# Layer 2 of a graph network: gathered rows added by VectorE into PSUM instead of by TensorE

## The chip, the cores and the metric

One NeuronCore of a Trainium2 chip runs the whole program. The metric is the time of one execution on the device in microseconds (us). All tensors are float32 unless said otherwise.

## The reference, cut to what matters

Four graph layers run one after the other on 3125 nodes of width 64, with 100000 edges that are sorted by destination. The change is inside layer 2:

```
xs = x[start]                                   # source row of each edge
h  = relu(concat(xs, x[end]) @ We1 + be1)       # 100000 x 128
e  = sigmoid(h @ We2 + be2)                     # one gate per edge
m  = e * xs                                     # message, width 64
m_sum = segment_sum(m, end);  m_max = segment_max(m, end)
... a small network on the nodes: (m_max, m_sum, x) -> x_out
```

## The kernel before, in words

**Layout.** The padded edges lie as 128 partitions x T = 784 columns, and a partition's edges are consecutive. A group is K = 8 columns, so there are NG = 98 groups. Loops over groups are written by `quads` (L127): six groups in line, then a loop whose body holds four groups, so that buffer numbers are constants.

**What layer 2 needs per edge.** The product with We1 is taken per node beforehand: the table `tab2` has, for each node, its source half of the product (128 wide) and the row itself (64 wide), and `put2` has the destination half, non-zero only at the first edge of each destination. Four groups of buffers rotate: `g2` for gathered rows (8 x 192), `z2` for destination rows (8 x 128).

**The engines in layer 2, for group g with slot s = g % 4:**

- SyncE (SP queue): `load_group` (L624) loads the ring of indices, waits until group g-4's destination rows are filled and added (`filled2`, `summed2`), and loads `z2` (L633, 512 KB); then `load2` (L634) clears part of layer 3's table (L491, 1040 KB).
- GpSimd: `gather2` (L802) waits for the ring, `summed2` and `made2` of group g-4, and issues eight indirect DMAs (L718), one column of 128 rows each.
- VectorE: `edges2` (L2260) is one stretch per group. For each of the eight columns k it runs `fill` (L1790), which spreads the destination's row to all its edges: z[k] = z[k-1] * ns + z[k], 128 wide, in SBUF; then one piece of older work: `relu2` of group g-2 after column 1 (L2231), `reduce2` of group g-2 after column 3 (L2238), and for each column the two instructions of `sum2` of group g-3 (L2252 and L2256, the running sum and maximum of the messages, 64 wide).
- TensorE: `add_up` (L1357) adds the gathered and the filled rows into two banks of PSUM by two products with the identity each (L1366, L1367), after `got` (gather landed), `filled2` and `work2`.
- `relu2` reads that sum from PSUM, applies relu, multiplies by we2 and writes `pr2` in SBUF; `reduce2` sums it to one score per edge.
- ScalarE: `gate` (L1039) applies the sigmoid (L1045), then writes the eight messages `m2` to SBUF (L1048), 64 wide each, and raises `made2`. It also stores the running sums (`keep2`, L1037).

Each instruction of VectorE is preceded by register and wait instructions on its own sequencer: `Beats` (L93) computes the value waited for, and `mark` computes the address of the column's marker. These show in the trace as DVEq.

**The order around the change.** VectorE's program is one fixed order per group, as listed. A slot comes free for GpSimd when ScalarE's messages of group g-4 are out. Softmax semaphores of layer 3 (`total_in`, `logged`, `inverse`) exist only there.

Of the kernel before, what the change touches and what calls it, by code (L numbers as in the profile page):

```python
# [21 lines left out]
ALU = mybir.AluOpType  # L22
# [6 lines left out]
P = 128  # L29
# [125 lines left out]
def gnn_program(nc, x, src, dst, etype, adj_v, deg_v, w0, b0, deg_coeff, coeff_param, scale_param,  # L155
# [3 lines left out]
    with ExitStack() as ctx:  # L159
# [176 lines left out]
        g2, z2, hold2 = quad(0, W2), quad(6200, HID), area(10300, HID)  # L336
        pr2, e2, m2, st2 = area(10500, K, HID), area(11600, 4, K), pair(11700, D), pair(12800, 2 * D)
        agg2 = area(17100, NT, 2 * D)
# [58 lines left out]
        apart1 = sem("apart1")  # L397
        filled2, summed2, work2, gate2, made2, scan2 = (sem(n) for n in ("filled2", "summed2", "work2", "gate2", "made2", "scan2"))
        filled3, summed3, work3, scored = (sem(n) for n in ("filled3", "summed3", "work3", "scored"))
# [3 lines left out]
        soft_in, soft_exp = sem("soft_in"), sem("soft_exp")  # L403
        total_in, logged, inverse = sem("total_in"), sem("logged"), sem("inverse")
        c_tail, c_turn, c_scan, c_back, c_in = (sem(n) for n in ("c_tail", "c_turn", "c_scan", "c_back", "c_in"))
# [105 lines left out]
        def _(sp):  # L511
# [111 lines left out]

            def load_group(n, put_rows, rows, filled_to, summed, g, s, uses):  # L624

                again = not isinstance(g, int) or g >= 4
                ring_load(n, g, s, *(((got[s], (uses[0] + past(n, s)) * 16 * K),) if again else ()))
                if again:
                    sp.wait_ge(filled_to, (g - 3) * K + 1)
                    sp.wait_ge(summed, g - 3)  # L630
                    if n == "3a":
                        sp.wait_ge(work3, (g - 4) * STEPS3 + READS3)
# [19 lines left out]

            quads(sp, lambda g, s, uses: load_group("3a", put3, z3, filled3, summed3, g, s, uses))

# [15 lines left out]
        def _(pool):  # L670
# [170 lines left out]
        def _(act):  # L841
# [259 lines left out]
            for r in range(H):  # L1101
                act.wait_ge(total_in, r + 1)
                act.activation(inv3[:, r, :], f3[:, r, :], ACT.Ln).then_inc(logged, 1)
            for r in range(H):
                act.wait_ge(logged, r + 1)
                act.activation(inv3[:, r, :], inv3[:, r, :], ACT.Exp, scale=-1.0).then_inc(inverse, 1)

# [15 lines left out]
        def _(pe):  # L1123
# [233 lines left out]
            def add_up(n, rows_of, banks, per_bank, width, g, s, uses, filled, steps, used, each, reads, summed):  # L1357
# [127 lines left out]
        def _(dve):  # L1485
# [737 lines left out]
            dve.wait_ge(hold_in, 16 * (PIECES + 2))  # L2223
            fills2, beats2, scans2 = Beats(dve, filled2, K), Beats(dve, work2, 2), Beats(dve, scan2, 2 * K)
# [15 lines left out]
            def sum2(g, s, uses, k):  # L2240

                h = s % 2
                if k == 0:
                    scans2.group(g)
                    dve.wait_ge(made2, g + 1)
                    if late(g, 2):
                        before = (s - 2) % 4
                        dve.wait_ge(states_out[before], (before_of(g, s, uses, 2)[0] + (1 + states_before(1, before))) * 16)
                start = isinstance(g, int) and g == 0 and k == 0
                prior = st2[:, h, k - 1, :] if k else st2[:, 1 - h, K - 1, :]  # L2250
                scans2.wait(1 if k else 0)
                scans2.add(dve.scalar_tensor_tensor(out=st2[:, h, k, 0:D], in0=zero[:, 0:D] if start else prior[:, 0:D],  # L2252
                                                    scalar=mark(ns, g, k), in1=m2[:, h, k, :],
                                                    op0=ALU.mult, op1=ALU.add))
                scans2.wait(1)
                scans2.add(dve.scalar_tensor_tensor(out=st2[:, h, k, D:2 * D], in0=lowest[:, :] if start else prior[:, D:2 * D],  # L2256
                                                    scalar=mark(neg, g, k), in1=m2[:, h, k, :],
                                                    op0=ALU.add, op1=ALU.max))
# [13 lines left out]
            for g in range(NG - 3, NG):  # L2272
                if g > NG - 3:
                    relu2(g, g % 2)
                    reduce2(g, g % 2)
# [142 lines left out]
            def total_done(r):  # L2418
                step(dve.tensor_scalar(f3[:, r, :], f3[:, r, :], 1e-16, None, ALU.max))
                dve.sem_inc(total_in, 1)  # L2420

            head_totals(6, "max", rest_of_maximum, neg, neg_last, late3, from_maximum)
            head_totals(10, "sum", sum_forward, ns, nl, first_last[:, :], total_done)
            for r in range(H):
                dve.wait_ge(inverse, r + 1)
                step(dve.tensor_tensor(f3[:, r, :], f3[:, r, :], inv3[:, r, :], ALU.mult))
# [103 lines left out]
```

## Time and profile before

| | us |
|---|---|
| median of 3 runs | 7645.4 |
| range of the runs | 7613.19 to 7655.54 |
| the profiled execution's own time | 7577.06 |
| its span | 7575.3 |
| layer 2's edge loop, from the first gather to the last message sum | 4207.6 to 5583.1 |

Over the span VectorE is busy for 3908.5 us (52%), GpSimd 3549.2 (47%), TensorE 2801.8 (37%) and ScalarE 1046.5 (14%). The numbers are of one execution of the program, recorded by the profiler. Times inside are counted from the start of the span. The loop over layer 2's edges takes about 18% of the span.

### The profile page before, as it was taken

The page shows a single profiled execution, that of the slowest core. Times are in us where ns is not written, and L with a number is a line of the kernel's source. Part 1 is how long each engine was busy: PE and PEld are TensorE (multiplying, and loading weights), DVE is VectorE, ACT ScalarE, POOL GpSimd, SP SyncE. Part 2 cuts the span into 40 slices and gives each one's busy share as a digit, 9 for nine tenths or more (in the row PEclk, how much of TensorE's full clock was granted, in tenths as well). Part 3 has the DMA queues.
Part 4 walks back from the last instruction along what each step waited for, and adds up shares of the span by engine and source line. Part 5 has one row for each costly group of instructions (what it writes and reads, how often), then busy time and mean ns, then how long its engine had stood idle before and what let it go on. Part 6 is the DMA issues. An engine that isn't in the chain of part 4 may idle for free. (4 is left out here: it accounts for less than half of the span.)

```text
span 7575.3 us, 62622 instructions
## 1 busy us (share of the span) xinstructions
PE 2801.8 (37%) x10703; PEld 1391.0 (18%) x10703; DVE 3908.5 (52%) x10542; ACT 1046.5 (14%) x2423; POOL 3549.2 (47%) x3645
## 2 busy tenths in 40 slices
PE   2116200057710000192002344333445655665694
PEld 1114100012300000181001111111122222222232
DVE  4218200399700000199865465555545666667995
ACT  0000000012200000181253111111110000000332
POOL 5650577400177777500002655555536666665463
PEclk9999999987755555596555677667677788787897
DMA  8100000045331111100242666666637777776693
GB/s 314 44 22 9 14 1 0 0 174 218 133 92 48 48 47 48 31 0 0 82 149 76 209 215 214 202 200 211 216 108 239 245 247 249 249 247 224 221 333 111
DMA packets 458410, 1039.70 MB, mean 137 GB/s; under 512 B 129581, under 2 KB 247829, under 8 KB 428140
## 3 DMA queue, kind: packets, MB, share of 16 engines
q1 hardware_dynamic: 167594, 579.38, 21.6%
q0 software_dynamic: 131968, 217.09, 10.5%
q10 hardware_dynamic: 158658, 241.42, 9.1%
q14 instruction: 159, 1.30, 0.1%
q8 instruction: 31, 0.51, 0.0%
HBM read 559.03 MB, written 476.15 MB: 137 GB/s over the span
## 5 line engine op out<-in xcount | busy, mean ns | idle before, releaser
L718 POOL DMA_INDIRECT arena<-tab,ring x2352 | 2334.7, 993 | 1345.8 <-issue 1104.9
L1366 PE MATMUL psum<-arena,ident 128*128 128x512 f32 x1176 | 760.1, 734 | 1369.5 <-DVE arena L1796 1198.0
L1796 DVE SCALAR_TENSOR_TENSOR arena<-arena,ns 128x64 f32<-128x64 f32 (+2 forms) x2351 | 874.6, 372 | 451.3 <-issue 304.2
L760 POOL DMA_INDIRECT weights<-arena x784 | 788.9, 1006 | 365.7 <-issue 312.7
L1941 DVE SCALAR_TENSOR_TENSOR arena<-iota_row,base,psum 128x200 f32<-128x200 f32 x784 | 278.4, 419 | 1082.1 <-remote 566.3
L1367 PE MATMUL psum<-arena,ident 128*128 128x512 f32 x1176 | 695.3, 677 | 0.0
L1330 PE MATMUL psum<-agg,arena 128*128 128x200 bf16 x2352 | 261.8, 267 | 1048.5 <-issue 623.0
L1366 PEld LDWEIGHTS psum<-arena,ident 128*128 128x128 f32 x1176 | 257.5, 234 | 1763.8 <-issue 1264.1
L2355 DVE SCALAR_TENSOR_TENSOR arena<-psum,rowb 128x1024 f32<-128x1024 f32 x196 | 239.0, 1219 | 375.7 <-remote 363.0
L707 POOL DMA_INDIRECT put<-arena,zidx x75 | 73.5, 979 | 739.2 <-DVE arena L1909 630.5
L1330 PEld LDWEIGHTS psum<-agg,arena 128*128 128x128 bf16 x2352 | 210.0, 104 | 1086.7 <-issue 627.4
L1448 PE MATMUL psum<-arena,ident 128*128 128x512 f32 x784 | 362.1, 608 | 54.0 <-DVE arena L2447 53.7
L830 POOL TENSOR_TENSOR arena<-arena,score 128x256 f32<-128x256 f32 x294 | 232.4, 815 | 249.3 <-issue 124.1
L1585 DVE SCALAR_TENSOR_TENSOR arena<-psum,arena,upper 128x128 bf16<-128x128 f32 x784 | 227.2, 348 | 224.6 <-remote 183.9
L1367 PEld LDWEIGHTS psum<-arena,ident 128*128 128x128 f32 x1176 | 264.0, 225 | 364.5 <-issue 364.5
L1748 DVE TENSOR_TENSOR nodev<-psum,nodev 128x25 f32<-128x25 f32 x98 | 17.4, 177 | 549.9 <-remote 445.0
L1240 PE MATMUL psum<-arena 128*128 128x25 bf16 x784 | 38.4, 185 | 683.3 <-DVE arena L1758 540.6
L735 POOL DMA_INDIRECT arena<-betas,eidx x25 | 24.9, 998 | 567.7 <-DVE score L2128 557.4
L2256 DVE SCALAR_TENSOR_TENSOR arena<-arena,neg 128x64 f32<-128x64 f32 x783 | 219.3, 280 | 130.2 <-issue 122.4
L937 ACT ACTIVATE psum<-psum,own_row 128x512 f32<-128x512 f32 x196 | 129.8, 662 | 1116.1 <-remote 716.9
L2252 DVE SCALAR_TENSOR_TENSOR arena<-arena,ns 128x64 f32<-128x64 f32 x783 | 221.1, 282 | 120.1 <-issue 92.9
L2362 DVE TENSOR_REDUCE arena<-arena 128x8 f32<-128x512 f32 x392 | 265.8, 679 | 0.1
(431 smaller groups left out, 4685.8 us busy)
## 6 DMA issues: line engine op xcount, KB each, us to landing
put<-zero SPq DMA_DIRECT2D x98, 1040.0 KB
arena<-put SPq DMA_DIRECT2D x98, 1040.0 KB
spill<-arena ACTq DMA_DIRECT2D x98, 1024.0 KB
arena<-spill SPq DMA_DIRECT2D x98, 1024.0 KB
state<-arena ACTq DMA_DIRECT2D x147, 512.0 KB
weights<-zero SPq DMA_DIRECT2D x32, 1600.0 KB
arena<-weights SPq DMA_DIRECT2D x32, 1600.0 KB, 7.3
put<-zero SPq DMA_DIRECT2D x14, 3584.0 KB
```

The lines of the kernel that those rows point to most:

```text
L718: pool.indirect_dma_start(out=rows[:, h, k, :], out_offset=None, in_=table[:, :], in_offset=bass.IndirectOffsetOnAxis(ap=ring[:, h, word + ...
L760: pool.indirect_dma_start(out=weights0[:, :], out_offset=bass.IndirectOffsetOnAxis(ap=words0[:, g, k:k + 1], axis=0), in_=words0f[:, g, K ...
L830: message = pool.tensor_tensor(y3[:, s % 2, k, :].rearrange("p (h c) -> p h c", c=D), gc3[:, s, k, 0:HD].rearrange("p (h c) -> p h c", c=D ...
L1330: mm = pe.matmul(bank(2 + 2 * h + k // 2)[:, k % 2 * NT * R:(k % 2 + 1) * NT * R], lhsT=picks[:, h, k, :], rhs=s_parts[:, a, :], start=(a ...
L1366: pe.matmul(place, lhsT=ident[:, :], rhs=rows_of[0][:, s, columns, 0:width], start=True, stop=False)
L1367: mm = pe.matmul(place, lhsT=ident[:, :], rhs=rows_of[1][:, s, columns, 0:width], start=False, stop=True)
L1448: mm = pe.matmul(bank(h).rearrange("p (c k) -> p k c", k=K), lhsT=ident[:, :], rhs=y3[:, h, :, head * D:(head + 1) * D], start=(head == 0) ...
L1585: marked = dve.scalar_tensor_tensor(out=alike[:, h * 4 + k, :], in0=bank(h)[:, k * P:(k + 1) * P], scalar=key[:, column], in1=upper[:, :], ...
L1796: beats.add(dve.scalar_tensor_tensor(out=rows[:, s, k, :], in0=before, scalar=mark(ns, g, k), in1=rows[:, s, k, :], op0=ALU.mult, op1=ALU. ...
L1941: pick = dve.scalar_tensor_tensor(out=sifted[:, h * 4 + k, :], in0=iota_row[:, :], scalar=src_column[:, column], in1=bank(2 + 2 * h + k // ...
L2355: beats3.add(dve.scalar_tensor_tensor(out=pr3[:, columns, :], in0=bank(4 * h + 2 * part, 2).rearrange("p (k c) -> p k c", c=HD), scalar=0. ...
L2362: beats3.add(dve.tensor_reduce(rs3[:, columns, :], pr3[:, columns, :].rearrange("p k (h c) -> p k h c", c=D), AX.X, ALU.add))
```

## The change

TensorE takes no part in layer 2's loop any more. `fill2` writes the filled destination rows to PSUM (`ends2_up`, two banks for even and two for odd groups), taking the previous row from there too. `add2`, at the head of `edges2`, waits for the gather (`got`) and writes gathered + filled rows of group g-2 to `pr2`, which is now in PSUM (two banks). `relu2` works on `pr2` in place, `reduce2` reads it there. The messages `m2` are in PSUM as well, one bank for each parity. `summed2` is gone, SyncE waits for `filled2` of group g-4 alone, ScalarE waits for `scan2` before it writes messages. Three semaphores of layer 3's softmax are folded into two others with other counts.

```diff
+        ends2_up = [bank(2 * h, 2).rearrange("p (k c) -> p k c", c=HID) for h in range(2)]
+        m2 = [bank(4 + h).rearrange("p (k c) -> p k c", c=D) for h in range(2)]
+        pr2 = bank(6, 2).rearrange("p (k c) -> p k c", c=HID)
...
             def load2(g, s, uses):
-                load_group("2", put2, z2, filled2, summed2, g, s, uses)
+                load_group("2", put2, z2, g, s, uses, (filled2, (g - 3) * K))
...
             def gather2(g, s, uses):
                 ready((ring_in[s], (uses[0] + past("2", s)) * 16 + 16),
-                      *(((summed2, g - 3), (made2, g - 3)) if not isinstance(g, int) or g >= 4 else ()))
+                      *(((made2, g - 3),) if not isinstance(g, int) or g >= 4 else ()))
...
-                act.wait_ge(work2, g * 2 + 2)
+                act.wait_ge(work2, g * 3 + 3)
                 act.activation(e2[:, 2 + h, :], e2[:, h, :], ACT.Sigmoid, bias=par[:, 6:7]).then_inc(gate2, 1)
                 act.wait_ge(gate2, g + 1)
+                if not isinstance(g, int) or g >= 2:
+                    act.wait_ge(scan2, (g - 1) * 2 * K)
                 for k in range(K):
-                    message = act.activation(m2[:, h, k, :], g2[:, s, k, HID:W2], ACT.Copy, scale=e2[:, 2 + h, k:k + 1])
+                    message = act.activation(m2[h][:, k, :], g2[:, s, k, HID:W2], ACT.Copy, scale=e2[:, 2 + h, k:k + 1])
...
-            quads(pe, lambda g, s, uses: add_up("2", (g2, z2), 2, 4, HID, g, s, uses, filled2, K, work2, 2, 1, summed2))
...
-            def relu2(g, h):
+            def add2(g, s, use):
                 beats2.group(g)
                 beats2.wait()
-                dve.wait_ge(summed2, g + 1)
-                beats2.add(dve.scalar_tensor_tensor(out=pr2, in0=bank(2 * h, 2).rearrange("p (k c) -> p k c", c=HID), scalar=0.0,
-                                                    in1=spread(row["we2"].unsqueeze(1), P, K, HID), op0=ALU.max, op1=ALU.mult))
+                dve.wait_ge(got[s], (use + past("2", s)) * 16 * K + 16 * K)
+                beats2.add(dve.tensor_tensor(pr2, g2[:, s, :, 0:HID], ends2_up[s % 2], ALU.add))
+            def relu2():
+                beats2.wait()
+                beats2.add(dve.scalar_tensor_tensor(out=pr2, in0=pr2, scalar=0.0, in1=spread(row["we2"].unsqueeze(1), P, K, HID),
+                                                    op0=ALU.max, op1=ALU.mult))
...
+            def fill2(g, s, k):
+                h = s % 2
+                if k == 0:
+                    fills2.group(g)
+                fills2.wait()
+                before = ends2_up[h][:, k - 1, :] if k else hold2 if isinstance(g, int) and g == 0 else ends2_up[1 - h][:, K - 1, :]
+                fills2.add(dve.scalar_tensor_tensor(out=ends2_up[h][:, k, :], in0=before, scalar=mark(ns, g, k), in1=z2[:, s, k, :],
+                                                    op0=ALU.mult, op1=ALU.add))
             def edges2(g, s, uses):
+                if late(g, 2):
+                    add2(g - 2, (s - 2) % 4, before_of(g, s, uses, 2)[0])
+                    beats2.wait()
                 dve.wait_ge(loaded[s], uses[0] * 16 + 16 * (1 + after("2", s)))
                 for k in range(K):
-                    fill(fills2, z2, hold2, g, s, k)
+                    fill2(g, s, k)
                     if late(g, 2) and k == 1:
-                        relu2(g - 2, s % 2)
+                        relu2()
```

In `sum2`, `in1` becomes `m2[h][:, k, :]` in both instructions; the three groups after the loop call `add2` and `relu2` for g > NG - 3.

## Rows read from the trace of the kernel before

**Rows 1.** Windows: us, busy (instructions) of PE, PEld, DVE, ACT, POOL; PEclk, DMA, GB/s.

```profile
4224.00:5584.00 1360.00, 519.21 (x785) 200.71 (x783) 779.82 (x2533) 227.25 (x882) 739.72 (x771) 0.69 0.61 205
4862.40:4869.00 6.60, 6.00 (x8) 2.07 (x7) 6.60 (x23) 2.17 (x9) 5.05 (x6) 0.62 0.41 139
4869.00:4885.00 16.00, 3.69 (x8) 1.44 (x8) 2.29 (x8) 0.15 (x1) 10.14 (x11) 0.77 0.88 294
4885.00:4891.80 6.80, 0.37 (x1) 0.38 (x2) 6.78 (x23) 2.32 (x9) 0.00 (x0) 0.50 0.09 30
4458.20:4461.00 2.80, 2.80 (x4) 1.21 (x4) 0.00 (x0) 0.00 (x0) 2.19 (x3) 0.50 0.57 203
4461.00:4469.20 8.20, 2.77 (x6) 1.07 (x5) 7.73 (x26) 2.32 (x9) 5.77 (x7) 0.92 0.73 227
```

**Rows 2.** Lines by form, 4300 to 5500: xcount, busy, mean ns, idle before, releasers.

```profile
L718 POOL DMA_INDIRECT arena<-tab,ring x684 | 656.5, 960 | 544.2 <-issue 542.4 <-PE psum L1367 1.8
L1796 DVE SCALAR_TENSOR_TENSOR arena<-arena,ns 128x128 f32<-128x128 f32 x691 | 239.8, 347 | 239.7 <-issue 236.9 <-DVE arena L2256 1.8
L2252 DVE SCALAR_TENSOR_TENSOR arena<-arena,ns 128x64 f32<-128x64 f32 x691 | 195.1, 282 | 98.9 <-issue 82.3 <-DVE arena L1796 10.3 <-DVE arena L2231 2.7
L1048 ACT ACTIVATE arena<-arena 128x64 f32<-128x64 f32 x688 | 173.5, 334 | 2.8
L2231 DVE SCALAR_TENSOR_TENSOR arena<-psum,rowb 128x1024 f32<-128x1024 f32 x86 | 105.1, 1222 | 44.8 <-issue 42.5
L2238 DVE TENSOR_REDUCE arena<-arena 128x8 f32<-128x1024 f32 x86 | 104.4, 1213 | 14.5 <-issue 12.4 <-DVE arena L1796 2.1
```

**Rows 3.** Waits, 4300 to 5500: waiter, releaser, total us, times, longest.

```profile
ACT arena L1045 <- DVE arena L2238: 860.2, 72, 19.7
POOL arena L718 <- issue: 542.4, 678, 12.3
POOL arena L718 <- PE psum L1367: 1.8, 6, 0.3
```

**Rows 4.** Timeline, 4881 to 4892: start, us, instruction, idle before.

```profile
4881.24 0.95 POOL L718 DMA_INDIRECT arena<-tab,ring  x1 [0.30 <-issue]
4885.02 1.23 DVE L2231 SCALAR_TENSOR_TENSOR arena<-psum,rowb 128x1024 f32<-128x1024 f32 x1 [1.75 <-issue]
4887.47 1.21 DVE L2238 TENSOR_REDUCE arena<-arena 128x8 f32<-128x1024 f32 x1
4888.72 0.30 ACT L1045 ACTIVATE arena<-arena,par 128x8 f32<-128x8 f32 x1 [19.57 <-DVE arena L2238]
4889.05 2.02 ACT L1048 ACTIVATE arena<-arena 128x64 f32<-128x64 f32 x8
4891.84 1.00 POOL L718 DMA_INDIRECT arena<-tab,ring  x1 [9.66 <-issue]
```

**Rows 5.** Source view of L2231, whole run: ns min/median/max, first and last start.

```profile
L2231 DVE SCALAR_TENSOR_TENSOR arena<-psum,rowb x98: 1209/1224/1226, 4230.0 to 5575.0; 128x1024 f32<-128x1024 f32 x98
```

**Rows 6.** Source views, L718 and L556, layer 1's gather (2093 to 3115).

```profile
L718 POOL DMA_INDIRECT arena<-tab,ring x744: 940/947/1935, 2093.3 to 3114.3; - x186
L556 SPq DMA_DIRECT2D ring<-meta x92: 6/700/1397, 2114.3 to 3105.4; - x92
```

**Rows 7.** Lines by form in other stages: PSUM and SBUF operands.

```profile
L2109 DVE TENSOR_TENSOR psum<-arena,psum 128x784 f32<-128x784 f32 x8 | 7.8, 979 | 0.3
L2174 DVE TENSOR_TENSOR xn<-xn,psum 128x320 f32<-128x320 f32 x5 | 2.4, 488 | 7.6 <-remote 7.3
L2196 DVE TENSOR_TENSOR xn<-xn,agg 128x320 f32<-128x320 f32 x5 | 2.4, 483 | 0.0
L2136 DVE SCALAR_TENSOR_TENSOR psum<-arena,ns,psum 128x64 f32<-128x64 f32 x96 | 31.5, 328 | 0.0
L937 ACT ACTIVATE psum<-psum,own_row 128x512 f32<-128x512 f32 x170 | 112.6, 662 | 147.8 <-remote 75.8 <-issue 43.6 <-PE psum L1319 28.3
L941 ACT ACTIVATE arena<-psum 128x512 bf16<-128x512 f32 x170 | 101.5, 597 | 12.0
```

More of the change, by code:

```diff
@@ L336, in gnn_program @@
         g2, z2, hold2 = quad(0, W2), quad(6200, HID), area(10300, HID)
-        pr2, e2, m2, st2 = area(10500, K, HID), area(11600, 4, K), pair(11700, D), pair(12800, 2 * D)
+        e2, st2 = area(11600, 4, K), pair(12800, 2 * D)
+        ends2_up = [bank(2 * h, 2).rearrange("p (k c) -> p k c", c=HID) for h in range(2)]
+        m2 = [bank(4 + h).rearrange("p (k c) -> p k c", c=D) for h in range(2)]
+        pr2 = bank(6, 2).rearrange("p (k c) -> p k c", c=HID)
         agg2 = area(17100, NT, 2 * D)
@@ L397, in gnn_program @@
         apart1 = sem("apart1")
-        filled2, summed2, work2, gate2, made2, scan2 = (sem(n) for n in ("filled2", "summed2", "work2", "gate2", "made2", "scan2"))
+        filled2, work2, gate2, made2, scan2 = (sem(n) for n in ("filled2", "work2", "gate2", "made2", "scan2"))
         filled3, summed3, work3, scored = (sem(n) for n in ("filled3", "summed3", "work3", "scored"))
@@ L403, in gnn_program @@
         soft_in, soft_exp = sem("soft_in"), sem("soft_exp")
-        total_in, logged, inverse = sem("total_in"), sem("logged"), sem("inverse")
         c_tail, c_turn, c_scan, c_back, c_in = (sem(n) for n in ("c_tail", "c_turn", "c_scan", "c_back", "c_in"))
@@ L622, in _, with load_group @@
             sp.wait_ge(rows_out, 16 * (1 + NBATCH))
-            def load_group(n, put_rows, rows, filled_to, summed, g, s, uses):
+            def load_group(n, put_rows, rows, g, s, uses, *free):
                 again = not isinstance(g, int) or g >= 4
@@ L628, in load_group @@
                 if again:
[L629 to L632, printed above, removed]
+                    for semaphore, value in free:
+                        sp.wait_ge(semaphore, value)
                 sp.dma_start(rows[:, s, :, :], group_rows(put_rows, g)).then_inc(loaded[s], 16)
             def load2(g, s, uses):
-                load_group("2", put2, z2, filled2, summed2, g, s, uses)
+                load_group("2", put2, z2, g, s, uses, (filled2, (g - 3) * K))
                 clear_columns(sp, put3, g * K, K, 2, zero3_out)
@@ L651, in _ @@
             sp.wait_ge(tab_out, 16 * (1 + 3 * NBATCH))
-            quads(sp, lambda g, s, uses: load_group("3a", put3, z3, filled3, summed3, g, s, uses))
+            quads(sp, lambda g, s, uses: load_group("3a", put3, z3, g, s, uses, (filled3, (g - 3) * K + 1), (summed3, g - 3), (work3, (g - 4) * STEPS3 + READS3)))
             def load3c(g, s, uses):
@@ L1101, in _ @@
             for r in range(H):
-                act.wait_ge(total_in, r + 1)
-                act.activation(inv3[:, r, :], f3[:, r, :], ACT.Ln).then_inc(logged, 1)
+                act.wait_ge(soft_in, 3 + H + r + 1)
+                act.activation(inv3[:, r, :], f3[:, r, :], ACT.Ln).then_inc(soft_exp, 1)
             for r in range(H):
-                act.wait_ge(logged, r + 1)
-                act.activation(inv3[:, r, :], inv3[:, r, :], ACT.Exp, scale=-1.0).then_inc(inverse, 1)
+                act.wait_ge(soft_exp, 3 + H + r + 1)
+                act.activation(inv3[:, r, :], inv3[:, r, :], ACT.Exp, scale=-1.0).then_inc(soft_exp, 1)
             pass_sums(1, work3c, run3, reset3, state3, st3)
@@ L2223, in _ @@
             dve.wait_ge(hold_in, 16 * (PIECES + 2))
-            fills2, beats2, scans2 = Beats(dve, filled2, K), Beats(dve, work2, 2), Beats(dve, scan2, 2 * K)
-            def relu2(g, h):
+            fills2, beats2, scans2 = Beats(dve, filled2, K), Beats(dve, work2, 3), Beats(dve, scan2, 2 * K)
+            def add2(g, s, use):
                 beats2.group(g)
                 beats2.wait()
-                dve.wait_ge(summed2, g + 1)
-                beats2.add(dve.scalar_tensor_tensor(out=pr2, in0=bank(2 * h, 2).rearrange("p (k c) -> p k c", c=HID), scalar=0.0,
-                                                    in1=spread(row["we2"].unsqueeze(1), P, K, HID), op0=ALU.max, op1=ALU.mult))
+                dve.wait_ge(got[s], (use + past("2", s)) * 16 * K + 16 * K)
[4 more added lines that the diff above has]
+                                                    op0=ALU.max, op1=ALU.mult))
             def reduce2(g, h):
@@ L2252, in sum2 @@
                 scans2.add(dve.scalar_tensor_tensor(out=st2[:, h, k, 0:D], in0=zero[:, 0:D] if start else prior[:, 0:D],
-                                                    scalar=mark(ns, g, k), in1=m2[:, h, k, :],
+                                                    scalar=mark(ns, g, k), in1=m2[h][:, k, :],
                                                     op0=ALU.mult, op1=ALU.add))
@@ L2273, in _ @@
                 if g > NG - 3:
-                    relu2(g, g % 2)
+                    add2(g, g % 4, g // 4)
+                    relu2()
                     reduce2(g, g % 2)
@@ L2419, in total_done @@
                 step(dve.tensor_scalar(f3[:, r, :], f3[:, r, :], 1e-16, None, ALU.max))
-                dve.sem_inc(total_in, 1)
+                dve.sem_inc(soft_in, 1)
             head_totals(6, "max", rest_of_maximum, neg, neg_last, late3, from_maximum)
@@ L2424, in _ @@
             for r in range(H):
-                dve.wait_ge(inverse, r + 1)
+                dve.wait_ge(soft_exp, 3 + 2 * H + r + 1)
                 step(dve.tensor_tensor(f3[:, r, :], f3[:, r, :], inv3[:, r, :], ALU.mult))
```

2 lines of the change are left out of this document (1 added, 1 removed).

## The prediction

> **What bounds the kernel now.** I read the windows first. Layer 2's loop takes 1360 us, and no engine fills it: VectorE is busy for 780, GpSimd 740, TensorE 519, ScalarE 227 [rows 1]. So something goes round in a circle. The relu runs 98 times between 4230.0 and 5575.0 [rows 5], so a group costs 1345 / 97 = 13.87 us and a pair of groups 27.7.
>
> Next the waits and the timeline, for the circle's members. ScalarE waits for the reduction (860 us), GpSimd for something that the view calls issue (542 us), and for TensorE hardly at all: 1.8 us [rows 3]. The timeline shows what GpSimd's pause is: relu 4885.02, reduction 4887.47, sigmoid 4888.72, messages from 4889.05 to 4891.07, and then, after 9.66 us of idle time, the next gather at 4891.84 [rows 4]. GpSimd needs the messages of group g-4 before it gathers group g. It issues two groups in one run, since the second one's messages are ready by then: 16 gathers of 0.95 us with 0.30 between them [rows 4], 20.0 us, and pauses for 27.7 - 20.0 = 7.7. TensorE's addition is not in the circle. VectorE's way to the reduction is.
>
> Then the windows inside one pair, where the pause comes from [rows 1]. In the first 6.6 us of GpSimd's run VectorE is busy all the time with 23 instructions. In the next 16.0 us it gets only 8 instructions done, busy for 2.29 us; the idle time before them is put down to issue, not to any other engine [rows 2]. This stretch ends shortly after GpSimd's run. In the last 6.8 us it does 23 instructions again, among them the reduction. So beside gathers VectorE's own sequencer passes an instruction only every 16.0 / 8 = 2.0 us, against 6.78 / 23 = 0.29 us otherwise. It is not the instruction's operands alone: in layer 1's gather, where GpSimd issues nearly without a break, SyncE's DMA issues take 0.70 us at the median [rows 6], and they touch no tensor of an engine.
>
> When does the slow stretch begin? In the pair above 6.6 us after the first gather, after 23 instructions of VectorE. In another pair VectorE did nothing for the first 2.8 us and then 26 instructions in 8.2 us before it began, 11.0 us after the first gather [rows 1]. That looks like a number of instructions rather than a time. The sum depends on it.
>
> **The change part by part**, per group unless said otherwise.
>
> *Removed from TensorE:* eight records of products and their loads. They cost nothing on the path (1.8 us in [rows 3]), so they give nothing back. With `summed2` goes one wait of VectorE and one of SyncE. SyncE's load of destination rows and its clear start earlier by TensorE's addition, 519 / 98 = 5.3 us busy per group [rows 1]; the rows were there in time before. Gain 0 to 0.3 us per pair.
>
> *`add2`:* one instruction over 1024 elements. The nearest row is L2109, PSUM from SBUF and PSUM, 784 elements in 979 ns [rows 7]; relu's L2231 has 1024 elements in 1222 ns [rows 2]. I take 1.22 us, and 0.04 for the wait of the first fill on its end (an estimate: the reduction at 4887.47 ends at 4888.68, and the sigmoid starts 0.04 later [rows 4]): 1.26 us. The wait for `got` costs nothing: two groups' gathers are issued ahead, and if that cover were gone, all sixteen columns of fills and sums would stand behind it, and ScalarE's messages after them. Whole loop: 98 x 1.26 = 123 us of VectorE, if all of it were on the path.
>
> *Fills* (8) read and write PSUM. Lower bound: L2174, one operand in PSUM, against L2196, none: 488 - 483 = 5 ns. Upper bound: L2136, PSUM written at 64 elements, 328 ns [rows 7], against 282 for the like in SBUF (L2252, [rows 2]): 46 ns, though its elements are strided, so I go near the lower one, 10 ns. *Sums* (16) read PSUM: 5 to 46 ns, I take 5. *Relu and reduction:* relu reads PSUM already; 10 ns each. Together 0.18 us, at most 1.2. They are on the path where VectorE is, and what is queued behind each one is the next column.
>
> *Messages* (8) are now written to PSUM. The only rows are of other functions: 662 ns to PSUM, 597 to SBUF at 512 elements [rows 7]. I take 0, from +0.065 x 8 = +0.5 to the same below, since the other way round has no row. ScalarE's wait for `scan2` names sums of group g-2, which VectorE finishes one whole group earlier: 0. Were it late, the messages would wait and GpSimd behind them.
>
> The Trainium skill ("VectorE: DVE Perf Modes", § The TRN2 errata) gives VectorE a fixed part of 58 cycles from SBUF and 120 from PSUM. By it each newly PSUM-reading instruction (8 fills, 16 sums, the addition, the reduction) would cost 62 / 0.96 = 65 ns more, 26 x 65 ns x 98 = 165 us as an estimate. This trace shows 5 ns for it (L2174 against L2196), so the sum does not use the rule; with it the serial rival below would be near 7935.
>
> *On the path, per pair.* The two windows beside GpSimd's run pass 23 + 8 = 31 instructions. If the slow stretch begins by number, a long instruction in the first window only shortens the slow one: 1.4 us less at 2.0 us per instruction is 0.7 instruction moved to the last window, 0.2 us. The two additions and the waits they bring take some 2.5 of the 31 places: 2.5 x 0.29 = 0.7 us moved. In the last window up to the reduction stand four sums, two fills, relu and reduction: 0.1 us. The earlier loads and SyncE's shorter program: -0.3. Sum 0.7 us per pair, 49 x 0.7 = 34 us. After the loop two additions stand bare: 2.5 us. The folded softmax semaphores keep their waits: 0.
>
> Sum: +37 us on the profiled execution, 7577 to 7614. The median of the runs lies 68 us above that execution, so I add to the median: 7645 + 37 = 7682.
>
> **The rivals.**
>
> 1. *All of VectorE's new work is on the path (slower).* The slow stretch begins by time, 6.6 us after the first gather, and what doesn't fit before it comes after it. For it: VectorE is full in the first and the last window. Against: the second pair of [rows 1]. Price per group 1.26 + 0.18 = 1.44, x 98 = +141: 7786; with the upper PSUM bounds (1.26 + 1.2) +241: 7886. It decides once 1 us per pair or more lands in the last window.
>
> 2. *The slow stretch goes away (faster).* If it is VectorE's second tensor in SBUF that stands against GpSimd, then putting one of the two tensors of every instruction in PSUM removes it. GpSimd then runs at 8 x 1.25 = 10.0 us per group; VectorE needs 780 / 98 + 1.44 = 9.4 beside it. The loop takes 98 x 10.0 = 980, 365 less: 7280; half of that is 7463. For it: VectorE is slow just beside gathers. Against: SyncE is slow too [rows 6], and the relu, with its one tensor in PSUM, waited for issue just as well (42.5 us in [rows 2]). The Trainium skill ("SBUF — State Buffer", § SBUF: two separate sides) says that a VectorE instruction with two SBUF inputs and a GpSimd one that reads SBUF exclude each other through a shared port pair; that rule is this rival.
>
> 3. *Slightly faster:* messages at the lower bound (-0.5 per pair) and the SyncE gain in full, additions hidden: -30 to -50 us, 7605.
>
> 4. *The earlier loads collide.* 1.5 MB of SyncE's traffic now starts with GpSimd's run; if the slow stretch begins 3 us earlier for it, 10 instructions move, 2.9 us per pair, +140: 7785.
>
> **How the numbers follow.** Within 0.5% (38 us, about what a measurement of this kernel tells from no change) is 7607 to 7684; the forecast lies at its upper edge. Forecast, 7682, own range 7620 to 7740: 0.52, of which 0.32 same, 0.16 slower, 0.04 faster. Rival 1: 0.19, slower. Rival 2: 0.14, faster. Rival 3: 0.09, 0.05 faster and 0.04 same. Rival 4: 0.06, slower. Together faster 0.23, same 0.36, slower 0.41. The range runs from 7500, which leaves out most of rival 2 (0.1), to 7810, which leaves out the upper part of rivals 1 and 4 (0.1).
>
> **What would show it.** Right: no TensorE in the loop; the addition near 1.22 us; fills under 0.37 us; slow stretches as before, one per run of 16 gathers, with some 31 instructions before their end; GpSimd's pause about 8.4 us; relu starts 14.2 us apart. Wrong: a pause of 10 us or more (rival 1), gathers without pauses (rival 2), or a slow stretch that begins right with the run (rival 4). Fills above 0.40 us would break the PSUM prices.

## The result and the profile after

| | before, us | after, us |
|---|---|---|
| median of 11 runs each | 7645.4 | 7682.89 |
| range | 7613.19 to 7664.04 | 7666.47 to 7710.23 |
| span of the profiled execution | 7575.3 | 7680.2 |

The ratio is 1.0055, its 95% interval 1.0042 to 1.0068: slower by 37 us, where 37 us were predicted. The profiled execution of the kernel before lay 68 us below its median, that of the kernel after at its median, so the two spans differ by 105 us, of which only a part is the change. It is read by the loop: relu, one per group. This is the view by source line (durations are ns min/median/max, then the first and the last start in us). The first fence is of the kernel after:

```profile
L2237 DVE SCALAR_TENSOR_TENSOR psum<-psum,rowb x98: 1220/1223/1232, 4254.0 to 5667.2; 128x1024 f32<-128x1024 f32 x98
L1050 ACT ACTIVATE psum<-arena x784: 293/297/318, 4257.5 to 5671.8; 128x64 f32<-128x64 f32 x196
```

1413.2 / 97 = 14.57 us per group, against 13.87 in [rows 5]; 14.2 were expected. In a later comparison on a chip like the first, both kernels were traced again: c_before, and behind it c_after.

```profile
L2231 DVE SCALAR_TENSOR_TENSOR arena<-psum,rowb x98: 1208/1220/1226, 4242.4 to 5592.7; 128x1024 f32<-128x1024 f32 x98
```

```profile
L2237 DVE SCALAR_TENSOR_TENSOR psum<-psum,rowb x98: 1219/1222/1232, 4227.2 to 5631.8; 128x1024 f32<-128x1024 f32 x98
```

There it is 13.92 and 14.48 us per group, 54 us for the loop. That is more than the 27 us (7623.03 - 7596.14) by which the whole kernel got longer in that comparison. Lines by form of the kernel after, 4300 to 5500, with the columns of [rows 2]:

```profile
L718 POOL DMA_INDIRECT arena<-tab,ring x661 | 626.6, 948 | 577.5 <-ACT psum L1050 354.9 <-issue 222.6
L2273 DVE SCALAR_TENSOR_TENSOR psum<-psum,ns,arena 128x128 f32<-128x128 f32 x661 | 233.8, 354 | 133.1 <-issue 109.0 <-DVE psum L2232 18.8 <-remote 2.7
L2258 DVE SCALAR_TENSOR_TENSOR arena<-arena,ns,psum 128x64 f32<-128x64 f32 x661 | 180.2, 273 | 88.8 <-issue 78.5 <-DVE psum L2273 4.3 <-remote 3.1
L1050 ACT ACTIVATE psum<-arena 128x64 f32<-128x64 f32 x656 | 162.5, 300 | 9.4 <-DVE arena L2262 0.2
L2232 DVE TENSOR_TENSOR psum<-arena,psum 128x1024 f32<-128x1024 f32 x83 | 101.6, 1224 | 125.7 <-issue 125.1 <-DVE arena L2262 0.5
L2244 DVE TENSOR_REDUCE arena<-psum 128x8 f32<-128x1024 f32 x82 | 99.5, 1214 | 9.3 <-issue 9.3
```

The reader sees the prices: the addition takes 1.224 us (1.22 expected), a fill 354 ns against 347 in [rows 2] (+7, where +10 was taken), the reduction 1214 against 1213 (+1, where +10 was taken). Running sums, now fed from PSUM, take 273 ns against 282, and messages, now written to PSUM, 300 against 334: both faster, where 0 to slower was taken. The larger part of GpSimd's idle time, 354.9 of 577.5 us, is now named for what it is, ScalarE's messages.

One pair of groups, in the windows with the columns of [rows 1]: from the first gather to the slow stretch, the slow stretch, and from its end to the next gather.

```profile
4867.40:4876.00 8.60, 0.00 (x0) 0.00 (x0) 8.04 (x25) 2.28 (x9) 6.62 (x7) 0.50 0.92 313
4876.00:4890.10 14.10, 0.00 (x0) 0.00 (x0) 2.71 (x6) 0.00 (x0) 8.54 (x9) 0.50 0.66 222
4890.10:4897.30 7.20, 0.00 (x0) 0.00 (x0) 7.11 (x24) 2.28 (x9) 0.00 (x0) 0.50 0.00 0
```

The shape of [rows 1] is still there: VectorE full, then hardly passing an instruction, then full again. The first window is 2.0 us longer with nearly the same number of instructions (25 against 23), the slow one 1.9 us shorter with 6 instead of 8. The pair's last row is GpSimd's next gather, in the timeline:

```profile
4897.32 0.95 POOL L718 DMA_INDIRECT arena<-tab,ring  x1 [10.18 <-ACT psum L1050]
```

### The profile page after: what moved, and what is told of

Same layout as the page of the kernel before. It is cut to its first block and busy times, and to the rows that moved or that the text cites. A ratio compares the mean times of both kernels' runs of the same rounds, so it can differ in the third digit from the quotient of the medians.

```text
span 7680.2 us, 60961 instructions
## 1 busy us (share of the span) xinstructions
PE 2280.5 (30%) x9919; PEld 1190.7 (16%) x9919; DVE 4007.2 (52%) x10640; ACT 1042.7 (14%) x2423; POOL 3572.7 (47%) x3645
## 5 line engine op out<-in xcount | busy, mean ns | idle before, releaser
L718 POOL DMA_INDIRECT arena<-tab,ring x2352 | 2362.9, 1005 | 1388.1 <-issue 745.8
L1797 DVE SCALAR_TENSOR_TENSOR arena<-arena,ns 128x64 f32<-128x64 f32 (+1 forms) x1567 | 601.1, 384 | 193.3 <-issue 68.9
L1368 PE MATMUL psum<-arena,ident 128*128 128x512 f32 x784 | 450.3, 658 | 531.7 <-DVE arena L1797 489.8
L1369 PE MATMUL psum<-arena,ident 128*128 128x512 f32 x784 | 428.5, 630 | 0.0
L1449 PE MATMUL psum<-arena,ident 128*128 128x512 f32 x784 | 362.1, 608 | 53.6 <-DVE arena L2467 52.8
L2273 DVE SCALAR_TENSOR_TENSOR psum<-psum,ns,arena 128x128 f32<-128x128 f32 x783 | 277.0, 354 | 159.9 <-issue 128.1
L2262 DVE SCALAR_TENSOR_TENSOR arena<-arena,neg,psum 128x64 f32<-128x64 f32 x783 | 215.1, 275 | 116.5 <-issue 106.3
L1368 PEld LDWEIGHTS psum<-arena,ident 128*128 128x128 f32 x784 | 157.8, 210 | 759.1 <-DVE arena L2382 498.7
L2258 DVE SCALAR_TENSOR_TENSOR arena<-arena,ns,psum 128x64 f32<-128x64 f32 x783 | 213.5, 273 | 110.6 <-issue 88.5
```

The source lines that it names most:

```text
L718: pool.indirect_dma_start(out=rows[:, h, k, :], out_offset=None, in_=table[:, :], in_offset=bass.IndirectOffsetOnAxis(ap=ring[:, h, word + ...
L1368: pe.matmul(place, lhsT=ident[:, :], rhs=rows_of[0][:, s, columns, 0:width], start=True, stop=False)
L1369: mm = pe.matmul(place, lhsT=ident[:, :], rhs=rows_of[1][:, s, columns, 0:width], start=False, stop=True)
L1449: mm = pe.matmul(bank(h).rearrange("p (c k) -> p k c", k=K), lhsT=ident[:, :], rhs=y3[:, h, :, head * D:(head + 1) * D], start=(head == 0) ...
L1797: beats.add(dve.scalar_tensor_tensor(out=rows[:, s, k, :], in0=before, scalar=mark(ns, g, k), in1=rows[:, s, k, :], op0=ALU.mult, op1=ALU. ...
L2273: fills2.add(dve.scalar_tensor_tensor(out=ends2_up[h][:, k, :], in0=before, scalar=mark(ns, g, k), in1=z2[:, s, k, :], op0=ALU.mult, op1=A ...
```

## The experiments

Chips turned out to be of two kinds. On three of the five comparisons (the one of the result, and two more) the kernel before takes 7596 to 7645 us; on the other two 5002 and 5001. On the second kind no trace has a slow stretch, and GpSimd issues all 784 gathers of layer 2 without a pause of 3 us. Register instructions of VectorE's sequencer (DVEq, L111 computes the values waited for) in the view by source line, the kernel after on the first kind, then e3_late on the second:

```profile
L111 DVEq ALU_OP  x1970: 1/40/1408, 4322.3 to 5499.2; - x197
```

```profile
L111 DVEq ALU_OP  x1940: 40/40/45, 2351.4 to 3148.4; - x194
L558 SPq DMA_DIRECT2D ring<-meta x80: 492/502/509, 2358.1 to 3149.2; - x80
```

I read ratios only against the kernel before of the same comparison, and questions on the slow stretch only on the first kind. Where a table says "loop", it is from the first to the last gather of layer 2 in that kernel's trace.

| run | kind | before, us | this, us | ratio [95%] | loop, us |
|---|---|---|---|---|---|
| e1_thin | 2 | 5002.07 | 5016.76 | 1.0026 [1.0015, 1.0038] | 1022.3 |
| e2_none | 2 | 5002.07 | 5025.09 | 1.0044 [1.0030, 1.0057] | 1029.9 |
| e3_late | 2 | 5002.07 | 4980.02 | 0.9952 [0.9938, 0.9966] | 978.6 |
| e5_before_m_psum | 2 | 5002.07 | 4988.73 | 0.9972 [0.9960, 0.9984] | 985.8 |
| c_before | 1 | 7596.14 | 7588.52 | 0.9989 [0.9974, 1.0004] | 1342.0 |
| c_after | 1 | 7596.14 | 7623.03 | 1.0040 [1.0019, 1.0060] | 1390.5 |
| e7_late2 | 1 | 7596.14 | 7639.69 | 1.0058 [1.0045, 1.0071] | 1397.7 |
| e6_clear_after | 1 | 7596.14 | 7762.13 | 1.0223 [1.0209, 1.0236] | 1404.7 |
| e8_thin_again | 1 | 7627.28 | 7653.11 | 1.0037 [1.0021, 1.0052] | 1402.5 |
| e9_none_again | 1 | 7627.28 | 7606.18 | 0.9972 [0.9953, 0.9992] | 1369.4 |
| c_after_again | 1 | 7627.28 | 7660.14 | 1.0051 [1.0032, 1.0070] | 1401.3 |
| e10_before_m_psum_again | 2 | 5000.80 | 4983.14 | 0.9962 [0.9949, 0.9976] | 982.6 |

### The addition made thin, and taken away

```diff
-                beats2.add(dve.tensor_tensor(pr2, g2[:, s, :, 0:HID], ends2_up[s % 2], ALU.add))
+                beats2.add(dve.tensor_tensor(pr2[:, :, 0:8], g2[:, s, :, 0:8], ends2_up[s % 2][:, :, 0:8], ALU.add))
...
-                beats2.add(dve.scalar_tensor_tensor(out=pr2, in0=pr2, scalar=0.0, ...
+                beats2.add(dve.scalar_tensor_tensor(out=pr2, in0=g2[:, s, :, 0:HID], scalar=0.0, ...
```

> The changed kernel, but the addition covers 8 of 128 elements per edge (64 instead of 1024 in the instruction) and relu takes its input from the gathered rows instead of the sum. The number of instructions and waits stays; each addition is about 1.0 us shorter. (The destination's half of the product is left out.) Theory of the prediction, the slow stretch begins after a number of VectorE's instructions: the time of the addition is mostly hidden, so 0.2 us per pair comes back, 10 us in all: ratio to the kernel before 1.003 to 1.005. Rival, the slow stretch begins at a time: 98 x 1.0 us come back, ratio 0.990 to 0.993. Anything between divides the two.

Without an addition, that line goes, and `work2` counts two per group:

```diff
-                beats2.add(dve.tensor_tensor(pr2, g2[:, s, :, 0:HID], ends2_up[s % 2], ALU.add))
...
-            fills2, beats2, scans2 = Beats(dve, filled2, K), Beats(dve, work2, 3), Beats(dve, scan2, 2 * K)
+            fills2, beats2, scans2 = Beats(dve, filled2, K), Beats(dve, work2, 2), Beats(dve, scan2, 2 * K)
```

> As the kernel with the thin addition, but without the addition and its waits at all (26 instead of 27 VectorE instructions per group; the destination's half is left out). Theory by number: against the thin one, 2.5 places of 0.29 us per pair come back, 0.7 us x 49 = 35 us, ratio about 0.999. Rival by time: against the thin one only the short instruction and its waits, 98 x 0.25 = 25 us; with the thin one at 0.992 this gives 0.988. Against the kernel before, this one differs by the place of fills and messages only (and by TensorE's absence), so it also shows what these are worth: by the prediction's terms +5 us, ratio 1.001.

Both leave the destination's half out of the sum, so they are for timing only. Both first met a chip of the second kind, where the question has no object: there is no slow stretch to begin by number or by time. The ratio 1.0026 lies just below the range by number (1.003 to 1.005), far from the one by time, and still speaks for neither, and that the kernel without the addition was no faster than the thin one says only that VectorE isn't the bound there. So both ran again, beside the changed kernel.

> The kernel with the thin addition once more (8 of 128 elements per edge, relu from the gathered rows, the destination's half left out), because its first run fell on a chip without slow stretches. On a chip with them (the kernel before takes about 7600, sequencer instructions beside gathers 0.70 us): theory of the prediction, onset by number: only 10 us of 1.0 us x 98 come back, ratio 1.003 to 1.005. Rival, onset by time: the loop gets 98 us shorter than the changed kernel's 1390, ratio 0.990 to 0.993. On the other kind of chip: 1.003 again.

> The kernel without any addition once more, for the same reason. On a chip with slow stretches, by number: against the thin one 35 us less, ratio 0.998 to 1.000; by time: against the thin one 25 us less, ratio about 0.988. If pauses of about 10 us stay even here, the new pause comes neither from the addition's length nor from its count, but from the places of fills, messages and loads. On the other kind of chip: 1.004 again.

> The changed kernel as a control. On a chip with slow stretches 1.004 to 1.0055 as twice before. On one without: its first run there; if the addition is hidden behind GpSimd, 1.002 to 1.005 as with the thin one (loop 1020 to 1035 us); if VectorE is the bound there, 1.008 to 1.013 (loop over 1050 us).

Now on the first kind, all three beside each other. The thin addition takes 0.228 us instead of 1.22 (relu, which now reads the gathered rows in SBUF, is unchanged at 1.225):

```profile
L2232 DVE TENSOR_TENSOR psum<-arena,psum x82: 222/228/230, 4307.4 to 5490.6; 128x64 f32<-128x64 f32 x82
```

98 x 1.0 = 98 us of VectorE's time are gone, and 7 us come back (7660.14 - 7653.11, with intervals that allow some 20 us either way); the loop is as long as before, 1402.5 against 1401.3. Taking the thin instruction and its waits away then gives 47 us (7653.11 - 7606.18), more than making it thin did, though it ran for only 22 us in all. This is the theory by number; the rival by time asked for at most 0.993 and has 1.0037. The 47 us carry some 20 us either way too, so they do not tell the 35 expected by number from the 25 expected by time; it is the thin kernel that decides.

The windows of a pair in e8_thin_again show how, with the columns of [rows 1]:

```profile
4393.00:4400.30 7.30, 0.00 (x0) 0.00 (x0) 6.53 (x21) 1.97 (x8) 5.75 (x6) 0.50 0.92 312
4400.30:4413.00 12.70, 0.00 (x0) 0.00 (x0) 1.71 (x6) 0.33 (x2) 9.52 (x11) 0.50 0.82 268
```

The slow stretch begins 7.3 us after the first gather and 21 instructions in, in the changed kernel 8.6 us and 25. Over the runs of 16 gathers between 4290 and 5520 whose starts are never more than 2.0 us apart, I counted the instructions of VectorE by where they start (medians; a slow stretch runs from the first to the last sequencer instruction of 0.64 to 0.78 us on VectorE or SyncE):

| kernel | runs of 16 | onset after first gather, us | instructions before it | in it | after it | GpSimd's pause, us |
|---|---|---|---|---|---|---|
| before | 36 | 6.8 | 21 | 11 | 20 | 8.3 |
| c_before | 30 | 7.0 | 22 | 10 | 22 | 8.4 |
| after | 25 | 8.5 | 23 | 6 | 26 | 10.7 |
| c_after | 29 | 8.5 | 23 | 6 | 25 | 10.3 |
| e8_thin_again | 21 | 7.3 | 21 | 7 | 25 | 10.3 |
| e9_none_again | 14 | 7.0 | 24 | 10 | 19 | 7.4 |

The onset moves by 1.7 us with the length of the instructions, and the number before it stays at 21 to 24. (These are medians; single runs lie mostly between 12 and 29 instructions, and in three of e8_thin_again the stretch is there from the first gather on.) The table leaves out the runs with a longer break inside, and in e8_thin_again these are half. If only pauses above 3 us part the runs, that kernel has 41: in 18 of them the onset comes 10.3 us after the first gather, in the other 23 after 7.3 us, and the medians before it are 22 and 21 instructions. Two onsets 3 us apart at the same number are the plainest sign that the stretch does not begin at a time.

What the addition changes looks in the table like the next column: 11 or 10 instructions pass in the slow stretch without it, 6 or 7 with it. That does not hold for the thin one once its other runs are counted: 10 pass, and the pause is 9.4 us. For e9_none_again the same count gives 12 instructions and 6.9 us, from only 15 runs, since many others there are of 24 gathers. What holds for the whole loop is GpSimd's idle time in gaps above 1 us:

| kernel | idle in gaps above 1 us | gaps above 3 us | their mean, us | the gathers themselves, us |
|---|---|---|---|---|
| before, c_before | 368, 364 | 45, 42 | 7.9, 8.2 | 752, 752 |
| after, c_after, c_after_again | 435, 429, 437 | 40, 40, 43 | 9.8, 9.8, 9.4 | 743, 741, 743 |
| e8_thin_again | 431 | 45 | 9.0 | 755 |
| e9_none_again | 365 | 35 | 9.9 | 780 |

With an addition, thin or full, it is 429 to 437 us, without one 364 to 368. So the cost goes with the instruction and its waits, not with its length. In e9_none_again the long pauses are no shorter than in the kernels with an addition, but fewer, and of the 66 us less idle time only 33 come back in the loop (1402.5 to 1369.4), since the gathers themselves take 25 us more.

### SyncE's loads later, and its clears out of the loop

```diff
-                load_group("2", put2, z2, g, s, uses, (filled2, (g - 3) * K))
+                load_group("2", put2, z2, g, s, uses, (filled2, (g - 3) * K + 5))
```

> The changed kernel, but SyncE's load of destination rows waits for five more fills (of group g-3), so that load and clear start about 5 us later in VectorE's order, near where they stood before the change. Theory of the prediction: the place of these DMAs is worth nothing, 0 to 15 us either way, ratio 1.004 to 1.007. Rival 4 in part (the earlier traffic makes the slow stretch last or weigh more): GpSimd's pause goes back from 10.3 to about 8.4 us, 1.9 x 49 = 90 us less, ratio 0.993 to 0.998.

The same with + 2 in place of + 5:

> The changed kernel, but SyncE's load waits for two more fills instead of five. Theory of the place: most of the gain of the five-fill kernel is there already, ratio 0.995 to 0.998. Rival (the five-fill kernel's gain comes from elsewhere, or only from far later loads): ratio 1.002 to 1.005.

With the clears behind SyncE's last load:

```diff
                 load_group("2", put2, z2, g, s, uses, (filled2, (g - 3) * K))
-                clear_columns(sp, put3, g * K, K, 2, zero3_out)
             quads(sp, load2)
+            quads(sp, lambda g, s, uses: clear_columns(sp, put3, g * K, K, 2, zero3_out))
```

> The changed kernel, but the 98 clears of layer 3's table (1040 KB each) stand behind SyncE's last load instead of one behind each load. Layer 2's loop then carries 40 percent less traffic. Theory of the place by traffic (the early clear fills the DMA engines just when a gather should land): the loop comes down to about 980 us, or on a chip with slow stretches the pauses shrink by several us each. Rival (the order of SyncE's waits matters, not the bytes): loop as in the changed kernel. The total is longer either way, since the clears then stand before layer 3: by 102 MB at 200 to 300 GB/s, 340 to 500 us, less what lies beside the node stage.

> The changed kernel itself once more. On the chip of the first four experiments the kernel before takes 5002 us, no instruction of VectorE's or SyncE's sequencer takes 0.70 us, and GpSimd issues a column of layer 2 every 1.25 us nearly without a pause (986 us for the loop with messages in PSUM). If this run meets such a chip: theory of the place (SyncE's loads and clears that start a group's fills earlier cost something by themselves, the addition nothing): loop near 1022 us as with the thin addition, ratio 1.003 to 1.005. Rival of VectorE's load (the full addition makes VectorE the bound, 9.4 us busy per group and waits beside it): loop over 1050 us, ratio 1.008 to 1.013. On a chip where the kernel before takes about 7645: 1.0055 again.

> The kernel before once more, for its trace on the chip of this comparison. On a chip without slow stretches: layer 2's loop 980 to 990 us, no pauses of GpSimd. Ratio 1.000 by construction.

On the first kind neither helps. With two fills of delay the loop is 1397.7 us, without any clear in it 1404.7, and 1390.5 in c_after beside them. The traces show directly that rival 4 (early loads start the slow stretch) falls: SyncE's first load of a run starts 5.5 us after the first gather in the kernel before, 0.6 us ahead of it in the kernel after and 2.2 us behind it in e7_late2 (medians), and the stretch begins later in the kernel after, 8.5 us against 6.8, not earlier. With the clears gone from the loop and the loop no shorter, the idea that their 102 MB make the stretch falls too. Both predicted gains missed. The clears cost their own time where they were put: layer 3's first gather starts 280.6 us after layer 2's last one (5894.4 - 5613.8), in c_after 162.4 (5762.5 - 5600.1); the 340 to 500 us that I expected were too many.

On the second kind five fills of delay go with a good deal: 0.9952, against 1.0026 of the thin kernel, which has less to do. (The prediction's theory asked for 1.004 to 1.007 there and missed; the number of rival 4 in part, 0.993 to 0.998, was met, but with no slow stretch to shorten.) The loops are 978.6 and 1022.3 us. The view by source line of GpSimd's gathers shows where it is, e1_thin and then e3_late:

```profile
L718 POOL DMA_INDIRECT arena<-tab,ring x784: 942/946/2017, 2253.6 to 3275.9; - x196
```

```profile
L718 POOL DMA_INDIRECT arena<-tab,ring x784: 942/946/977, 2254.3 to 3233.0; - x196
```

The median gather is the same, but with the early loads some take up to 2.0 us, with the later ones none more than 0.98. GpSimd is the bound there (98 x 8 x 1.25 = 980 us), so each such gather costs in full: over the loop the gathers take 784.7 and 741.1 us, 43.6 less, and the loop is 43.7 shorter. Which of the transfers they meet is not shown. The changed kernel itself never met a chip of the second kind, so its ratio there is open, as is e3_late's on the first.

### The messages in PSUM alone

```diff
-        pr2, e2, m2, st2 = area(10500, K, HID), area(11600, 4, K), pair(11700, D), pair(12800, 2 * D)
+        pr2, e2, st2 = area(10500, K, HID), area(11600, 4, K), pair(12800, 2 * D)
+        m2 = [bank(4 + h).rearrange("p (k c) -> p k c", c=D) for h in range(2)]
```

This is the kernel before otherwise, with TensorE's addition.

> The kernel before, with one part of the change alone: ScalarE's messages lie in PSUM, and VectorE's sums read them there. In the changed kernel's trace a message takes 300 ns instead of 334 and a sum 275 instead of 282. If these were all on the path: 98 x (8 x 0.034 + 16 x 0.007) = 38 us less, ratio 0.995. By the prediction messages and sums are worth nothing or a little: the block of eight messages goes at nearly the same pace in both (1.98 and 2.02 us), so -4 us for the messages and -5 for the sums near the reduction: ratio 0.998 to 1.000. If sequencer time beside gathers rules, 1.000.

> The kernel before with ScalarE's messages in PSUM once more, since its first run (ratio 0.9972) fell on a chip without slow stretches. On a chip with them the kernel without an addition was 21 us faster than the kernel before, which the prediction's terms don't explain (+4 us). If that gain is the messages' and sums' (34 ns less per message, 7 ns less per sum, each on the way to GpSimd's release): ratio 0.996 to 0.998, and this version beats both kernels on both kinds of chip. If it came from TensorE's absence, the fills in PSUM or SyncE's earlier loads: 0.999 to 1.001.

It is faster twice, 0.9972 and 0.9962, both on the second kind. Messages and sums in it, by source line (e10_before_m_psum_again):

```profile
L1049 ACT ACTIVATE psum<-arena x784: 295/298/318, 2277.6 to 3249.2; 128x64 f32<-128x64 f32 x196
L2253 DVE SCALAR_TENSOR_TENSOR arena<-arena,ns,psum x783: 264/275/282, 2281.4 to 3252.2; 128x64 f32<-128x64 f32 x196
```

The prices per instruction are nearly those of the changed kernel (300 and 273 ns). The gain of 13 to 18 us is more than the 9 us I gave it at 0.998, less than "all on the path" (38 us). Where in the program it arises isn't shown, since no trace of the kernel before was taken on the second kind, and on the first kind the version wasn't measured. It is the version that beats the kernel before wherever it ran, and e3_late beats it by a little more there.

## Why the prediction was right, step by step

The number was met almost exactly; that is in part luck, as the terms below show. The direction, the circle and the onset by number stand.

*The circle.* Right. GpSimd waits for ScalarE's messages, 354.9 us by name in the kernel after, and TensorE's leaving the loop changed nothing that shows as a gain.

*The stretch begins by number.* Right, and this was the step on which the forecast and rival 1 parted. Shown by e8_thin_again (98 us of instruction time are worth 7) and by the counts, above all its two onsets 3 us apart at the same number.

*Where the places are lost.* The size was nearly right, the place was not what I described. I moved 2.5 places per pair into the last window at 0.29 us each. In the trace one of a pair's two group borders lies inside the slow stretch. In the kernel before, from the end of the last sum ahead of it (4870.96 + 0.28) to the start of the first sum behind its fill it takes 7.48 us; three rows of the timeline of that kernel, with the idle time before each in brackets:

```profile
4870.96 0.28 DVE L2256 SCALAR_TENSOR_TENSOR arena<-arena,neg 128x64 f32<-128x64 f32 x1 [1.11 <-issue]
4875.22 0.35 DVE L1796 SCALAR_TENSOR_TENSOR arena<-arena,ns 128x128 f32<-128x128 f32 x1 [3.98 <-issue]
4878.72 0.28 DVE L2252 SCALAR_TENSOR_TENSOR arena<-arena,ns 128x64 f32<-128x64 f32 x1 [3.15 <-issue]
```

The same in the kernel after, whose last sum ends at 4878.41:

```profile
4878.13 0.28 DVE L2262 SCALAR_TENSOR_TENSOR arena<-arena,neg,psum 128x64 f32<-128x64 f32 x1 [1.79 <-issue]
4880.26 1.23 DVE L2232 TENSOR_TENSOR psum<-arena,psum 128x1024 f32<-128x1024 f32 x1 [1.85 <-issue]
4885.22 0.36 DVE L2273 SCALAR_TENSOR_TENSOR psum<-psum,ns,arena 128x128 f32<-128x128 f32 x1 [3.73 <-issue]
4888.70 0.28 DVE L2258 SCALAR_TENSOR_TENSOR arena<-arena,ns,psum 128x64 f32<-128x64 f32 x1 [3.12 <-issue]
```

There it is 10.29 us: 2.8 more, about four steps of 0.70, for one instruction with its waits. The stretch ends with GpSimd's run, so these steps push some four instructions into the window behind it. At 0.29 us that is 1.2, and the pause of an unbroken run grew by 1.9 (8.4 to 10.3) instead of 0.7; the other 0.7 is not accounted for. Against that stand the pairs whose runs are split. Over the loop, the mean pause went from 7.8 to 9.0 us (2 x 13.92 - 20.0, 2 x 14.48 - 20.0) where 8.4 was predicted, and the changed kernel's loop is 54 us longer where 34 were. From the first to the last gather it is 48.5 us in that comparison (1342.0 and 1390.5) and 50 in the first traces (1349.0 and 1398.6), while the whole kernel became longer by 27 and 37 us by the medians. So the loop's term was too small by about a third, and the rest of the kernel made up for it. What did so is not shown: outside the loop two traces of one kernel differ by 19 us (before, c_before) and 56 (after, c_after).

*The terms of the sum*, in the comparison of e8 and e9:

| term | predicted, us | measured, us |
|---|---|---|
| length of the additions | +10 | +7 (thin to full) |
| the places of instructions and waits, with the tail | +34 + 2.5 | +47 (none to thin) |
| everything else (fills, sums, messages, SyncE) | +5 - 15 = -10 | -21 (before to none) |
| sum | +37 | +33; +37 in the result, +27 with c_after |

The differences of two medians carry intervals of some 15 to 20 us, so no term alone is refuted. The places came out larger, the rest lower, and the two errors point against each other: the closeness of 7682 to 7682.89 is better than the terms deserve. Nor is the -21 seen in a loop: that of e9_none_again takes 1369.4 us, and those of the kernel before, traced in two other comparisons, 1349.0 and 1342.0. (The expectations for e2_none and e10_before_m_psum_again gave "everything else" as +5 and +4 us; they left SyncE's -15 out.)

*PSUM prices.* Right for fills, relu, reduction and the addition, within 10 ns. Wrong in sign for sums and messages: the range for sums began at +5 ns, and -9 was measured for the running sum, -5 for the maximum; I took 0 for messages, and they are 34 ns shorter. The rule of 62 cycles more for an operand from PSUM ("VectorE: DVE Perf Modes", § The TRN2 errata of the Trainium skill) isn't seen in any of them.

*The rivals.* Rival 1 fell with e8_thin_again. One of its signs, a pause of 10 us or more, was there all the same in unbroken runs: the sign was badly chosen, as a pause can grow by count too. Rival 2 fell in the trace after, slow stretches being there as before with one tensor of each instruction in PSUM. Rival 3 may be in part real: the messages' 13 to 18 us on the second kind point to it, and the -21 on the first, whose place is open. Rival 4 fell on the first kind with the later onset, e7_late2 and e6_clear_after; on the second, e3_late's loop is 44 us shorter than the thin kernel's, by another mechanism.

## What to carry to other kernels

Where a sequencer is slow, an instruction is priced by its sequencer steps (itself, register computations, waits), not by its busy time: shortening an instruction by 1.0 us was worth 7 us in 98, and dropping what was left of it, 0.23 us with its waits, 47. Before trusting a time, look at how long register instructions take in the trace: on the two kinds of chip nearly the same kernel was bound by different things. Loads that start two fills later gave nothing on one kind, while loads that start five fills later went with 0.5% less time than the kernel before and 0.7% less than the thin kernel on the other (the changed kernel itself wasn't measured there). Where the engine that issues gathers is the bound, try whether a transfer that is "early enough" anyway does better when it starts late.

## What the runs showed of the hardware

- The same kernel takes 7596 to 7645 us on some chips and 5001 on others. In layer 2 the difference is the slow stretches (loop 1342 us, and 983 to 986 for nearly the same kernel on the second kind), in layer 3 likewise (1246.5 and 1013.2 us from the first to the last gather; 150 of VectorE's sequencer instructions take 0.64 to 0.78 us there in c_before, none in e5_before_m_psum). Most of the rest lies outside the edge loops and wasn't studied: 2102 against 1155 us before layer 1's first gather, 1037 against 115 between layer 1's last and layer 2's first (c_before and e5_before_m_psum).
- Beside GpSimd's gathers, on the first kind, sequencer instructions of VectorE and of SyncE take about 0.70 us in the slow stretches: in c_after 332 of VectorE's 544 there and 98 of SyncE's 273, while 166 of the other 212 of VectorE's take 25 ns or less. No instruction of GpSimd's or ScalarE's sequencer in layer 2's loop does. SyncE's load of the ring in layer 1 takes 0.70 us at the median on the first kind [rows 6] and 0.49 on the second, so of that 0.70 only 0.2 is the slowness.
- The stretch begins after some 22 instructions of VectorE whatever their length, and in the kernel after it ends a median 2.5 us behind the run. That is how a store of instructions fetched ahead would look that isn't refilled beside gathers; it is a guess. The Trainium skill ("Runtime: NRT & Kernel Launch", § Instruction fetch mechanics) describes such a store, filled through a DMA queue of each sequencer's own. In the traces the packets of the instruction queue (q14, 8 KB each) are as many in layer 2's loop on both kinds, 115 to 117, and as short, 0.33 to 0.39 us at the median: the transfers themselves are not slow. Whether they are asked for late, or something else holds the sequencers, and why only on some chips, no run here shows: the cause stays open.
- It isn't the traffic of clears: with over a third of the loop's bytes gone (1040 of some 2880 KB per group, 249.09 MB in 1200 us being 2.88 MB per 13.87), the loop was no shorter (1404.7 against 1390.5 us).
- A 128x64 activation takes 300 ns to PSUM and 334 to SBUF; a running sum of 128x64 on VectorE 273 ns with one operand from PSUM (276 in e8_thin_again) and 282 with both from SBUF.
